# Output projection moved ahead of the channel mixing products in a gated block, eight batches on one core

## The reference, cut to what matters

```python
# first part, per batch; emb = layernorm(x) + ctx
q, k, v = emb @ wq + bq, emb @ wk + bk, emb @ wv + bv
ek = exp(k - max_k);  ew = exp(w - max_w)
y = sigmoid(q) * (ew @ (ek * v)) / (ew @ ek)
a = layer_norm(y @ wo + bo + emb)                 # output projection: y @ wo
ff = relu(a @ w1 + b1) @ w2 + b2                  # hidden width 1024
x1 = x + tanh(g_xattn) * layer_norm(ff + a)
# second part: channel mixing; n = layernorm(x1), prev = n shifted by one row
xr = mu_r * n + (1 - mu_r) * prev;  xk = mu_k * n + (1 - mu_k) * prev
out = x1 + tanh(g_ffn) * sigmoid(xr @ W_r.T) * (relu(xk @ W_k.T) ** 2 @ W_v.T)
```

## Time and profile before

| | us |
|---|---|
| median of 3 runs | 478.46 |
| lowest and highest run | 475.48, 478.86 |
| the profiled execution's own time | 479.9 |
| its span | 478.2 |
| PE busy | 439.5 (92%) |
| DVE busy | 407.1 (85%) |
| POOL busy | 275.3 (58%) |
| ACT busy | 255.9 (54%) |

### The profile page before, as it was taken

One profiled execution on the slowest core, in us unless ns is written; L12 is line 12 of the kernel. 1 busy time (PEld: TensorE's weight loads), 2 busy tenths in 40 slices (PEclk: granted clock), 3 DMA queues, 4 the chain that ended last, 5 costly groups with the idle time before them and its releaser, 6 DMA issues.

```text
span 478.2 us, 8097 instructions
## 1 busy us (share of the span) xinstructions
PE 439.5 (92%) x2884; PEld 395.8 (83%) x2884; DVE 407.1 (85%) x761; ACT 255.9 (54%) x406; POOL 275.3 (58%) x224
## 2 busy tenths in 40 slices
PE   8989979975999899999999998998999997899985
PEld 8869879964989798897979796996989796897975
DVE  4998778969997989879997999699976997489887
ACT  3681652634487165835386256833485255638463
POOL 2574834465765766957865685846763572753521
PEclk9999989997999989999999999998999999999999
DMA  8741310156214632247214641254213321011002
GB/s 266 264 132 34 123 44 1 45 178 179 96 44 125 217 79 78 90 141 221 88 45 144 199 111 44 93 164 153 89 45 86 102 91 43 1 45 44 3 1 89
DMA packets 44217, 48.27 MB, mean 101 GB/s; under 512 B 8592, under 2 KB 40336, under 8 KB 44176
## 3 DMA queue, kind: packets, MB, share of 16 engines
q1 hardware_dynamic: 43088, 46.18, 30.9%
q10 hardware_dynamic: 1088, 1.57, 1.0%
HBM read 31.29 MB, written 16.45 MB: 100 GB/s over the span
## 4 chain that ended last, share of the span: by engine, by line
DVE 26%; PE 18%; issue 17%; DMA 14%; POOL 10%; ACT 9%; SPq 5%; ACTq 0%; DVEq 0%; POOLq 0%
PE ps L1719 17%; SPq L475 3%; DVE hid_lo L1071 3%; DVE y L923 3%; DMA sum_room<-sums_t 3%; DMA out_sb<-fin_room 3%; DMA fin_room<-xk 2%; POOL ek_lo L238 2%; POOL xk_lo L238 2%; DVE x L940 2%; ACT norm L1355 2%; DVE xk L867 2%; DMA key_room<-norm 1%; DMA hid<-in_wo 1%; SPq L495 1%
## 5 line engine op out<-in xcount | busy, mean ns | idle before, releaser
L1523 ACT ACTIVATE hid_hi<-ps,b 128x512 fp32r<-128x512 f32 x60 | 37.9, 684 | 45.2 <-PE ps L1719 45.2
L1719 PE MATMUL ps<-w_hi,hid_hi 128*128 128x256 f32 x248 | 61.3, 283 | 0.8 <-issue 0.5
L1719 PE MATMUL ps<-w_lo,hid_hi 128*128 128x256 f32 x248 | 60.8, 282 | 0.0
L1719 PE MATMUL ps<-a_hi,w_hi 128*128 128x512 f32 x128 | 52.5, 410 | 1.4 <-DVE hid_lo L1071 0.9
L923 DVE RECIPROCAL y<-y 128x512 f32<-128x512 f32 x16 | 53.5, 3346 | 0.3
L1719 PE MATMUL ps<-a_hi,w_lo 128*128 128x512 f32 x128 | 51.9, 406 | 0.0
L1719 PE MATMUL ps<-a_lo,w_hi 128*128 128x512 f32 x128 | 38.0, 422 | 12.9 <-DVE a_lo L238 12.9
L1719 PEld LDWEIGHTS ps<-w_hi,hid_hi 128*128 128x128 f32 x248 | 46.7, 188 | 1.7 <-issue 1.2
L1071 DVE SCALAR_TENSOR_TENSOR hid_lo<-ps,neg_b,hid 128x512 fp32r<-128x512 f32 x60 | 41.3, 735 | 7.3 <-ACT hid L1529 7.3
L1719 PEld LDWEIGHTS ps<-w_lo,hid_hi 128*128 128x128 f32 x248 | 46.7, 188 | 0.3
L238 POOL TENSOR_TENSOR ek_lo<-y,ek_hi 128x1024 fp32r<-128x1024 f32 x13 | 31.3, 2405 | 25.4 <-DVE x L949 16.7
(11 more groups left out here) (268 smaller groups left out, 1386.3 us busy)
## 6 DMA issues: line engine op xcount, KB each, us to landing
x_in<-in_x SPq DMA_DIRECT2D x8, 512.0 KB, 4.1
emb<-in_ctx SPq DMA_DIRECT2D x8, 512.0 KB, 4.1
x_beta<-in_x SPq DMA_DIRECT2D x8, 512.0 KB, 4.0
out<-out_sb SPq DMA_DIRECT2D x7, 512.0 KB, 3.8
mid_room<-hid SPq DMA_DIRECT2D x6, 512.0 KB, 2.6
hid<-mid_room SPq DMA_DIRECT2D x24, 128.0 KB, 2.8
key_room<-norm SPq DMA_DIRECT2D x6, 512.0 KB, 2.7
y<-key_room SPq DMA_DIRECT2D x24, 128.0 KB, 2.8
```

Of the source, the lines that this page charges most:

```text
L1523: act.activation(tile(hi, b, T), bank(relu_pair(n, q), b), ACT.Relu, bias=b1[:, m:m + 1]).then_inc(hid_hi_done, 1)
L1719: return pe.matmul(o, s, m, start=start, stop=stop, skip_group_check=True)
```

## The change

The output projection is issued right behind `hidden(b, 2)`, ahead of `ffn_k(a)` and `ffn_r(a)`. The pairs are set for it: `ffn_k` takes pair 1 (in steps 2 to 6), so it waits until the keys have been read (`ek_done`), and `ffn_r` takes pair 2, which the output projection has just filled, so it waits for `attention_sum` (`res_done`). The orders of DVE, ACT, POOL and SP are rewritten for it, and step one has an order of its own (`first_step`). Every engine issues the same operations as before, in another order.

```diff
         def k_pair(n):
 
-            return 0 if n >= BATCH - 3 else 2
-
-        def r_pair(n):
-
-            return 2 if n >= BATCH - 3 else 1
+            return 0 if n >= BATCH - 3 else 1
...
                 elif not is_last(i):
                     spread_keys(i + 1)
-                    spread_sums(i + 1)
                     if has(i + 2):
                         load_ctx(i + 2, p)
                     spread_mid(i)
-                    sp.wait_ge(mid_landed, mid_moved(i))
+                    spread_sums(i + 1)
...
             def step(i, p):
                 a, b, d, e = i - 2, i - 1, i + 1, i + 2
-                if has(a):
+                if not has(a):
+                    first_step(i, p)
+                    return
+                if a > 0:
                     pool.wait_ge(norm_done["fin"], TT * (a + 1))
                 ev_low(i)
-                if has(d) and d >= FIRST_EMB:
+                if has(d):
                     emb_square_low(pool, d)
                 finish_a(b, 1 - p)
                 if has(d):
                     emb_plus_bo(d, 1 - p)
-                if has(a):
-                    pool.wait_ge(xr_done, DC * (a + 1))
-                    xk_low(pool, a)
-                    xr_low(pool, a)
+                x_plus_beta(b)
+                pool.wait_ge(xk_done, DC * (a + 1))
                 y_low(pool, i)
+                xk_low(pool, a)
+                xr_low(pool, a)
...
+                stats("mid", i)
+                sq_low(pool, a)
+                scale_a(i, p)
                 if has(e):
-                    pool.wait_ge(norm_done["mid"], TT * (i + 1))
                     make_emb(pool, e, p)
-                if i != FIRST_MID:
-                    scale_a(i, p)
-                if i != FIRST_MID and not is_last(i):
-                    pool.wait_ge(out_done, a + 1)
-                    x_plus_beta(b)
+                if has(d):
+                    ek_low(pool, d)
                 if is_last(i):
                     finish_a(i, p)
                 stats("ff", b)
-                if has(d):
-                    pool.wait_ge(x1_done, TT * (b + 1))
-                    ek_low(pool, d)
                 stats("fin", b)
 
...
+            def first_step(i, p):
...
+                hidden_low(b, 3)
+                turn_key_squares(d)
+                ff_sum(b, 1 - p)
+                ff_stats(b)
+                sum_keys(d)
+                scale_ff(b)
+                a_square_low(dve, i)
+                finish_x1(b)
+                fin_stats(b)
+                turn_emb_squares(e, p)
+                keep_values(d)
...
             def step(i, p):
                 a, b, d, e = i - 2, i - 1, i + 1, i + 2
                 if i < FIRST_EK:
                     sums_low(i, 0)
+                    first_step(i, p)
+                    return
...
-                if has(a):
-                    mix_k(a)
-                    mix_r(a)
+                mix_k(a)
                 if has(d):
                     key_max(d)
...
             def ffn_k(n):
                 if n < BATCH - 3:
-                    pe.wait_ge(y_done, DC * (n + 3))
+                    pe.wait_ge(ek_done, DC * (n + 4))
                 elif n == BATCH - 3:
                     relus_read(NQ * (n + 1) + 1)
                 channels_out(k_pair(n), unit(6, 0), xk_hi, xk_lo, xk_lo_done, n + 1, fk_done, xk_hi_done, DC * n)
 
             def ffn_r(n):
-                if n < BATCH - 3:
-                    pe.wait_ge(ek_done, DC * (n + 4))
-                else:
-                    pe.wait_ge(y_done, DC * BATCH)
+                pe.wait_ge(res_done, min(n + 3, BATCH))
                 pe.wait_ge(mu_r_done, DC * (n + 1))
                 pe.wait_ge(xr_hi_done, n + 1)
                 hi, lo = xr_split(n)
-                rows_out(r_pair(n), unit(6, 1), hi, lo, xr_lo_done, n + 1, fr_done)
+                rows_out(2, unit(6, 1), hi, lo, xr_lo_done, n + 1, fr_done)
 
             def ffn_v(n, before_low=None):
                 pe.wait_ge(sq_hi_done, n + 1)
                 if n < BATCH - 3:
-                    pe.wait_ge(tanh_r_done, n + 1)
+                    pe.wait_ge(sq_done, n + 1)
                 else:
                     relus_read(NQ * (n + 2) if n == BATCH - 2 else NQ * (n + 1) + 3)
                 rows_out(value_pair(n), unit(7, 0), sq_hi, sq_lo, sq_lo_done, n + 1, fv_done, before_low=before_low)
...
                 keys(d)
                 relus_read(NQ * b + 1)
                 hidden(b, 2)
+                pe.wait_ge(y_hi_done, i + 1)
+                rows_out(2, unit(1, 1), y_hi, y_lo, y_lo_done, i + 1, wo_done)
                 if has(a):
                     if a == 0:
                         for u in (6, 7):
                             pe.wait_ge(w_lo_done[u], 1)
                     ffn_k(a)
                     ffn_r(a)
-                    pe.wait_ge(sq_done, a + 1)
-                pe.wait_ge(y_hi_done, i + 1)
-                rows_out(2, unit(1, 1), y_hi, y_lo, y_lo_done, i + 1, wo_done)
-                pe.wait_ge(ek_done, DC * (d + 1))
-                if has(a):
                     relus_read(NQ * b + 3)
+                else:
+                    pe.wait_ge(ek_done, DC * (d + 1))
                 hidden(b, 3)
                 if has(a):
                     ffn_v(a)
                 add_hidden(b, 2)
                 add_hidden(b, 3)
-                pe.wait_ge(res_done, i + 1)
+                if has(a):
+                    pe.wait_ge(tanh_r_done, a + 1)
+                else:
+                    pe.wait_ge(res_done, i + 1)
                 queries(d, 2)
                 if has(a):
                     pe.wait_ge(gated_done, a + 1)
...
 
                 pe.wait_ge(den_read, DC * BATCH)
                 hidden(b, 2)
+                pe.wait_ge(y_hi_done, i + 1)
+                rows_out(2, unit(1, 1), y_hi, y_lo, y_lo_done, i + 1, wo_done)
                 ffn_k(a)
                 ffn_r(a)
                 pe.wait_ge(sq_done, a + 1)
-                pe.wait_ge(tanh_r_done, a + 1)
-                pe.wait_ge(y_hi_done, i + 1)
-                rows_out(2, unit(1, 1), y_hi, y_lo, y_lo_done, i + 1, wo_done)
                 hidden(b, 3)
                 ffn_v(a)
                 add_hidden(b, 2)
                 pe.wait_ge(norm_done["mid"], TT * (i + 1))
+                pe.wait_ge(tanh_r_done, a + 1)
                 turn(2, norm, mid_turned)
                 add_hidden(b, 3)
                 pe.wait_ge(gated_done, a + 1)
```

More of the change, by code:

```diff
@@ L1137, in _, with first_step @@
             dve.wait_ge(dve_const, 5)
+            def first_step(i, p):
+                b, d, e = i - 1, i + 1, i + 2
+                gate_den(i, 0)
+                gate_den(i, 1)
+                recip(i, 0)
+                emb_low(d)
+                sums_low(i, 1)
+                recip(i, 1)
+                make_y(i)
+                key_max(d)
+                head_stats(e)
+                unit_low(6)
+                unit_low(7)
+                attention_sum(i, p)
+                hidden_low(b, 2)
+                normalise_mid(i)
+                turn_mid_squares(i)
+                hidden_low(b, 3)
[9 more added lines that the diff above has]
+                keep_values(d)
+                weigh_values(d)
+                sums_low(d, 0)
+                hidden_low(i, 0)
+                hidden_low(i, 1)
+                normalise_fin(b)
+                turn_fin_squares(b)
             def step(i, p):
@@ L1167, in step @@
+                if has(d):
+                    turn_key_squares(d)
+                if has(e):
+                    head_stats(e)
+                attention_sum(i, p)
+                square(a)
+                hidden_low(b, 2)
+                normalise_mid(i)
+                if not is_last(i):
                     turn_mid_squares(i)
-                    hidden_low(b, 3)
-                    head_stats(e)
-                    turn_key_squares(d)
+                hidden_low(b, 3)
+                gate_ffn(a)
@@ L1171, in step @@
+                make_out(a)
+                if has(d):
                     sum_keys(d)
-                else:
-                    if has(e):
-                        head_stats(e)
-                    if has(d):
-                        turn_key_squares(d)
-                    square(a)
-                    if has(d):
-                        sum_keys(d)
-                    hidden_low(b, 2)
-                    attention_sum(i, p)
-                    if not is_last(i):
-                        normalise_mid(i)
-                        turn_mid_squares(i)
-                    hidden_low(b, 3)
-                    if is_last(i):
-                        normalise_mid(i)
```

150 lines of the change are left out of this document (64 added, 86 removed).

## The result

| | before | the change |
|---|---|---|
| median of the runs | 478.66 us (4 runs) | **487.04 us** (4 runs, 486.63 to 488.89) |
| ratio | | 1.0204, interval 1.0153 to 1.0255 |
| profiled execution, span | 479.9, 478.2 | 487.41, 485.7 |
| steps 2 to 6 together | 266.65 | 281.32 |

The account below looks back on a forecast made before the run. PE was taken to set the time (92% busy), DVE close behind (85%). Terms -5.5 (step one), +12.2 (steps 2 to 6) and -1 (step seven) sum to +5.7 on 478.46: 484.2 us, range 465 to 490.

Parts of the forecast that it names:

- the mechanism: Steps 2 to 6: POOL holds DVE's blends; res_done at T + 28.0 (T: step's first matmul), PE idles 3.5 us.
- step one: First step: a_lo comes earlier, its 6.0 us wait and half clock go; -5.5 us, bounds 7.7 to 4.2 less.
- step seven: Last stretch: new 1.9 us wait for y_hi halves the clock, other waits go; -1 us, between -3 and +1.5.
- the sum of steps 2 to 6: Five middle steps: 278.8 us against 266.65 before, +12.2, at 55.5 a step and some 1.5 more for step 2.
- 1.7 for a spell at half clock: PE after a long wait: cost taken per spell at 1.2 GHz, between 1.0 and 2.9 us.
- the copying of step 4 to all five: Steps 2 to 6: each taken at step 4's forecast of 55.5 us, all five 277.3.
- The upper bound of 2.9: PE after a long wait: most that a half-clock spell costs, as one more block of 2.87 us would.
- its 57.0: Step 2: the 55.5 us plus some 1.5 (estimate, 0 to 2.4), since POOL comes into it late.
- B: Rival, steps 2 to 6: blends not held at all, res_done at T + 24.3; 463.6 us, chance 0.18.
- C: Rival: steps 2 to 6 stay as they are, only step one gives; 472 us, chance 0.24 together with A.
- D: Rival: something costed at nothing (DMA round trips, sq_low) comes late, 1 us a step; 489 us, chance 0.14 with the rest.
- A: Rival: POOL does not get between mix_r's halves, res_done T + 25.8; 471.1 us, chance 0.24 together with C.

Follow-up runs that it names:

- Experiment 1: Changed kernel, with POOL's xk_low again waiting until both blends are done (xr_done): 477.16 us, 1.0027 of before.
- experiment 8: Changed kernel, with x_plus_beta on POOL moved behind ek_low and nothing else: 484.83 us, 1.0179 of before.
- Experiment 4: Kernel before, with only the change's order of the first step on DVE, ACT and POOL, plus the wait it needs: 473.63 us, 0.9929 of before.
- experiment 12: Kernel of experiment 10, with x_plus_beta on POOL behind ek_low and a wait for make_out ahead of make_emb: 471.30 us, 0.9877 of before.
- 7: Kernel of experiment 5, with POOL's xk_low waiting for xr_done and x_plus_beta moved behind ek_low: 478.46 us, 1.0035 of before.
- 10: Kernel of experiment 9, with hidden_low(b, 2) ahead of square; on POOL x_plus_beta behind scale_a, head statistics ahead of xr_low: 474.16 us, 0.9938 of before.
- 2: Changed kernel, with attention_sum on DVE moved ahead of turn_key_squares and head_stats: 494.50 us, 1.0407 of before.
- 5: Changed kernel, with attention_sum, hidden_low(b, 2), square ahead of turn_key_squares and head_stats on DVE; mid statistics and sq_low ahead of head statistics on POOL: 481.94 us.
- 9: Changed kernel, with head_stats and turn_key_squares on DVE moved ahead of mix_r: 488.73 us, 1.0236 of before.
- 11: Kernel of experiment 10, with keep_values ahead of fin_stats on DVE: 474.72 us, 0.9960 of before.

## Why the prediction was right, and where its sizes were off

**Right: the mechanism, the place and the sign.** The held blends were forecast with their times. In step 4, forecast and measured: mix_k ends at T + 18.0 and 18.2; mix_r at T + 23.8 and 24.0; res_done at T + 28.0 and 28.0; PE's wait 3.5 and 3.34; hidden(b, 3) at T + 32.6 and 32.55; the step 55.5 and 55.44. Experiment 1 shows the cause of the long mix_r by itself (2.15 us, one wait on POOL), experiment 8 that of the long mix_k.

**Right: step one.** Forecast -5.5, step 2 starting at 111.9; it starts at 111.70, which is -6.1. The wait that was to come next, for keep_values, is there with 1.72 (1.6 forecast). Experiment 4 shows that this part stands by itself, though 1.4 us of it go again in step 2.

**Right: step seven.** The new wait for y_hi is 2.0 us (forecast 1.9) with a spell at half clock, the stretch 1.0 shorter, as forecast (485.7 - 393.02 = 92.7, before 478.2 - 384.49 = 93.7).

**Too small: the sum of steps 2 to 6**, +14.7 against +12.2. It is the term "1.7 for a spell at half clock" and the copying of step 4 to all five. Behind the waits of steps 3 and 5 the clock stays low twice as long as behind those of steps 2 and 4 (stretches of the change, the granted clock third from the end of the row; first step 3, then step 4):

```profile
198.00:200.00 2.00, 1.93 (x9) 1.93 (x10) 1.92 (x11) 0.36 (x1) 1.17 (x3) 0.50 0.40 123
...
203.00:204.00 1.00, 1.00 (x5) 0.90 (x5) 0.00 (x0) 0.40 (x1) 0.00 (x0) 0.53 0.04 15
204.00:205.00 1.00, 1.00 (x5) 0.80 (x5) 0.00 (x0) 1.00 (x2) 0.00 (x0) 1.00 0.00 0
...
255.00:257.00 2.00, 2.00 (x12) 2.00 (x11) 1.96 (x9) 0.00 (x0) 1.07 (x5) 0.53 0.68 194
257.00:258.00 1.00, 1.00 (x7) 1.00 (x6) 1.00 (x2) 0.00 (x0) 0.92 (x2) 0.50 0.84 223
258.00:259.00 1.00, 1.00 (x8) 1.00 (x8) 1.00 (x3) 0.00 (x0) 0.15 (x1) 0.73 0.94 312
```

In step 3 PE works from 198.07 to about 203.9 at 1.2 GHz, 5.9 us, which costs 2.9; in step 4 from about 255.1 to 258.5, which costs 1.7. So step 3 came out 1.1 and step 5 1.6 above the 55.5. The upper bound of 2.9 was in the text; I took 1.7 for all. Step 6 came out 1.5 below: it has no head statistics, since no batch is left to load, so res_done comes 1.5 us earlier, and its two waits of 1.66 and 1.50 leave the clock up. Copying step 4 to it was a slip.

Step 2 came out 1.2 above its 57.0, and that it came so near is in part luck. The forecast laid its lateness to POOL alone. But it is DVE that is held there, by the same mechanism: weigh_values takes 2.57 us for the 1.26 of before, and normalise_fin 2.43 for 0.73:

```profile
117.31 2.43 DVE L969 TENSOR_SCALAR norm<-x,rs_fin,nmr_fin 128x256 f32<-128x256 f32 x2
```

```profile
116.87 2.40 POOL L238 TENSOR_TENSOR ev_lo<-res,ev_hi 128x1024 fp32r<-128x1024 f32 x1 [1.09 <-ACT ev_hi L1444]
```

So sums_low is late, and PE waits 2.28 us for it at 126.02.

**Right in part: the rivals.** B (no holds) fell: the blends are held. C fell too: steps 2 to 6 do not stay as they are. D's total of 489 lies as near to the 487.0 as the forecast's 484.2, but not by its cause: PE waits for no DMA in steps 2 to 6, and for sq_low nowhere more than 0.3 us. A, that POOL waits its turn, is what experiment 1 builds, and PE's waits in the middle of a step (0.6, 0.4 and 1.15) are near the 0.9 and 1.3 of the text. hidden(b, 3) starts at T + 30.0 there, 1.7 later than before, as A has it.

The total is not A's: 471.1 forecast, 477.2 measured. Steps 2 to 6 take 272.95 us and not 265.8. Of these 7.1 us, 4.5 lie in step 2, which takes 58.86: a spell at half clock near its start costs 1.7, y_hi 1.27 and keep_values at its end 1.30. The rest is mostly keep_values again, 1.3 us in each of steps 3 and 5. There the step of A that failed is that a late keep_values costs nothing behind 20 us of PE's blocks. With PE earlier, DVE's list is as long as PE's own work of 50.6 us (its busy time in step 4 before; the 50.2 of my expectations was low): in experiment 12 it is 48.4 busy and 3.4 of DVE's own waits. What the prediction saw as a cover was PE's own lateness. The prediction did name this price (keep_values or sums_low, 1 us a step), but put it on top of the forecast and not on A.

**Why the change does not pay.** It takes PE's a_lo waits away (6.9 us in steps 2 to 6) and gives DVE 3.1 us more to stand in a step (47.4 busy in step 4 before, 50.5 after), because POOL's waits that kept it away from DVE's blends went with the reordering. Taken out one by one, the holds give it back. PE's new order is then worth little: steps 2 to 6 take 265.88 in experiment 12 and 267.23 with the old order in experiment 4, and the intervals of the two ratios overlap. What the new order would give with no hold left at all is not shown.

**Left open.** Step 2 takes 55.7 us in experiment 4 and 57.3 to 58.9 in experiments 1, 7, 10 and 12. Waits of 0.3 to 2.3 us for sums_low, y_hi and xk_lo stand there. One hold goes with it: normalise_fin takes 0.73 us in experiment 4, and 1.65, 2.50 and 2.26 in experiments 1, 10 and 12, where POOL's ev_low runs beside it. But no run took it out alone, and spells at half clock lie in the same step.

## What to carry to other kernels

Waits that look idle can be what keeps two engines off each other: before an engine's waits are reordered away, list which of its instructions will then run beside which of its neighbour's, and price the pairs that can't run together. When a late result is to be mended, follow every instruction that stands behind the same queue (here hidden_low, square, sq_low and keep_values, one after the other), on all engines; in experiments 1, 2, 5, 9 and 11 a wait that was taken away came back at another block. And compare the two fullest engines within one step, with their own waits: with PE at 50.6 and DVE at 48 to 50.5 us busy, a gain on one is soon capped by the other.
